# GpSimd makes the low parts of o's last 64 columns for nine pairs of heads in the middle of the output projection

## The reference, cut to what matters

```python
x = x + cross_attention(layernorm(x), ctx)      # 32 batches, 64 tokens, 16 heads of 64
x = x + rwkv_time_mix(layernorm(x), ...)        # k, v, r products, a scan over 64 tokens
x = x + feed_forward(layernorm(x), ...)         # 256 -> 1024 -> 256, relu
```

## Time and profile before

| | |
|---|---|
| median of 3 runs | 2353.97 us (2352.03 to 2357.43) |
| the profiled execution's own time | 2352.82 us |
| its span in the trace | 2351.0 us |
| PE busy | 2291.5 us, 97% of the span |
| DVE busy | 1812.6 us, 77% |
| ACT busy | 1542.7 us, 66% |
| POOL busy | 1646.7 us, 70% |

### The profile page before, as it was taken

How to read it: one execution, slowest core, us unless ns; L and a number is a source line. 1 busy time by engine, 2 the same in 40 slices (tenths; PEclk the granted TensorE clock), 3 DMA queues, 4 the chain that set the end, 5 groups by cost and what they waited for, 6 DMA issues and landing times.

```text
span 2351.0 us, 43942 instructions
## 1 busy us (share of the span) xinstructions
PE 2291.5 (97%) x13696; PEld 2097.1 (89%) x13696; DVE 1812.6 (77%) x3664; ACT 1542.7 (66%) x2696; POOL 1646.7 (70%) x858
## 2 busy tenths in 40 slices
PE   7979999999999999999999999999999999899999
PEld 5769999999999999999999999999999998878788
DVE  7867777777777777777777777777777777679884
ACT  6756666666666666666666666666666666565444
POOL 4238878888888888888888888888888886421111
PEclk9999999999999999999999999999999999999999
DMA  8988888888888888888888888888888886987000
GB/s 228 267 199 189 196 196 197 199 199 200 198 200 199 199 199 199 199 201 199 199 199 199 199 200 199 200 199 200 199 199 199 199 199 162 212 197 198 8 10 28
DMA packets 410273, 438.97 MB, mean 187 GB/s; under 512 B 82528, under 2 KB 380896, under 8 KB 410208
## 3 DMA queue, kind: packets, MB, share of 16 engines
q1 hardware_dynamic: 394384, 427.23, 77.3%
q10 hardware_dynamic: 15824, 10.91, 2.0%
HBM read 167.42 MB, written 52.43 MB: 94 GB/s over the span
## 4 chain that ended last, share of the span: by engine, by line
POOL 44%; issue 25%; PE 18%; SPq 5%; DVE 4%; DMA 2%; ACT 2%; POOLq 0%; ACTq 0%; DVEq 0%
POOL p_pt_lo L640 24%; POOL p_nat L667 7%; POOL p_q_lo L652 5%; POOL p_ct_lo L648 4%; POOL p_ct_hi L659 4%; SPq L441 3%; PE p_scores L1508 3%; PE p_scores L1678 2%; PE p_cols L1665 2%; PE p_scores L1632 2%; PE p_acc L1528 2%; PE p_cols L1574 2%; PE p_scores L1461 1%; DMA p_raw<-o_scratch 1%; PE p_scores L1590 1%
## 5 line engine op out<-in xcount | busy, mean ns | idle before, releaser
L640 POOL TENSOR_TENSOR p_pt_lo<-p_landed,p_pt_hi 128x768 fp32r<-128x768 f32 x504 | 991.1, 1987 | 322.7 <-ACT p_pt_hi L861 322.7
L1528 PE MATMUL p_acc<-p_nat,p_pt_hi 128*128 128x384 f32 x3024 | 887.6, 360 | 7.5 <-POOL p_pt_lo L640 5.7
L1530 PE MATMUL p_acc<-p_nat,p_pt_lo 128*128 128x192 f32 x3024 | 758.2, 251 | 0.0
L897 ACT ACTIVATE p_prob<-p_scores,p_negmax 128x800 f32<-128x800 f32 (+1 forms) x512 | 471.5, 926 | 392.8 <-DVE p_negmax L1222 392.7
L1508 PE MATMUL p_scores<-p_ct_hi,p_q_hi 128*128 128x512 f32 (+2 forms) x2048 | 703.6, 347 | 11.5 <-ACT p_prob L897 11.5
L1508 PE MATMUL p_scores<-p_ct_hi,p_q_lo 128*128 128x512 f32 (+2 forms) x2048 | 703.1, 347 | 0.0
L1528 PEld LDWEIGHTS p_acc<-p_nat,p_pt_hi 128*128 128x128 f32 x3024 | 567.4, 188 | 17.1 <-POOL p_pt_lo L640 10.1
L1530 PEld LDWEIGHTS p_acc<-p_nat,p_pt_lo 128*128 128x128 f32 x3024 | 577.0, 191 | 0.0
L861 ACT ACTIVATE p_pt_hi<-p_landed 128x768 fp32r<-128x768 f32 x504 | 398.6, 838 | 166.0 <-PE p_acc L1532 123.8
L1230 DVE STREAM_TRANSPOSE turned<-p_prob 128x1536 f32<-128x1536 f32 x256 | 452.5, 1768 | 0.0
L1508 PEld LDWEIGHTS p_scores<-p_ct_hi,p_q_hi 128*128 128x128 f32 x2048 | 389.0, 190 | 56.8 <-ACT p_prob L897 12.7
(11 more groups left out here) (229 smaller groups left out, 3126.2 us busy)
## 6 DMA issues: line engine op xcount, KB each, us to landing
p_landed<-turned SPq DMA_DIRECT2D x2032, 104.0 KB, 2.3
resid<-in_ctx SPq DMA_DIRECT2D x128, 288.0 KB, 5.0
o_scratch<-resid SPq DMA_DIRECT2D x256, 96.0 KB, 2.7
qk_scratch<-p_out_a SPq DMA_DIRECT2D x32, 512.0 KB, 5.1
p_stage<-qk_scratch SPq DMA_DIRECT2D x31, 512.0 KB, 3.8
p_stage<-qk_scratch SPq DMA_DIRECT2D x62, 256.0 KB, 4.2
p_stage<-in_ctxT SPq DMA_DIRECT2D x31, 401.0 KB, 4.7
p_stage<-in_ctxT SPq DMA_DIRECT2D x62, 200.5 KB, 5.6
```

The costliest lines, as they stand in the source:

```text
L640: nc.gpsimd.tensor_tensor(pt_lo[:, t0:t1, :, :], by_tile(slot, t0, t1), bits(pt_hi[:, t0:t1, :, :]), ALU.subtract).then_inc(pt_lo_done, 1)
L897: nc.scalar.activation(prob[:, lo:hi], scores[:, S0 + lo:S0 + hi], ACT.Exp, bias=negmax[:, par:par + 1], accum_out=rowsum[:, par, h:h + 1] ...
L1528: nc.tensor.matmul(acc[k % 2][:, 0:2 * DC], pt_hi[:, t, :, :].rearrange("p i x -> p (i x)"), x[:, t, :], start=t == 0, stop=False, skip_gr ...
L1530: nc.tensor.matmul(acc[k % 2][:, 0:DC], pt_lo[:, t, :, :].rearrange("p i x -> p (i x)"), x[:, t, 0:DC], start=False, stop=False, skip_grou ...
```

## The change

For the nine steps 13 to 21 the low part of `ob` is made on POOL instead of DVE. POOL does all nine between `to_mixed(0)` and `to_mixed(1)`, each as soon as `o_hi(n)` is done, and counts a new semaphore `ob_lo_done`. For these steps DVE's `o_lo(n)` is L1280 alone. Whoever waited for `o_lo_done` of such a step waits for both counters now: `v(n)` on PE and `load(n + 3)` on SP.

```diff
+        SHARED = range(13, 22)
+
+        def pair_split(eng, n):
+            eng.wait_ge(o_lo_done, n + 1)
+            if n in SHARED:
+                eng.wait_ge(ob_lo_done, n - SHARED.start + 1)
...
             def load(n):
-                sp.wait_ge(o_lo_done, n - RAW + 1)
+                pair_split(sp, n - RAW)
                 load_pair(sp, n)
...
+            def shared_lo(n):
+                s, r = n % 2, n % RAW
+                pool.wait_ge(o_hi_done, n + 1)
+                nc.gpsimd.tensor_tensor(ob_lo[s], ob[r], bits(ob_hi[s]), ALU.subtract).then_inc(ob_lo_done, 1)
+
-            to_mixed(0); to_mixed(1); to_x(2); to_x(3); to_mixed(2); to_fed(0); to_mixed(3); to_fed(1); to_fed(2); to_fed(3)
+            to_mixed(0)
+            for n in SHARED:
+                shared_lo(n)
+            to_mixed(1); to_x(2); to_x(3); to_mixed(2); to_fed(0); to_mixed(3); to_fed(1); to_fed(2); to_fed(3)
...
             def o_lo(n):
                 s, r = n % 2, n % RAW
                 dve.wait_ge(o_hi_done, n + 1)
-                nc.vector.tensor_tensor(oa_lo[s], oa[r], bits(oa_hi[s]), ALU.subtract)
-                nc.vector.tensor_tensor(ob_lo[s], ob[r], bits(ob_hi[s]), ALU.subtract).then_inc(o_lo_done, 1)
+                last = nc.vector.tensor_tensor(oa_lo[s], oa[r], bits(oa_hi[s]), ALU.subtract)
+                if n not in SHARED:
+                    last = nc.vector.tensor_tensor(ob_lo[s], ob[r], bits(ob_hi[s]), ALU.subtract)
+                last.then_inc(o_lo_done, 1)
...
             def v(n):
...
-                pe.wait_ge(o_lo_done, n + 1)
+                pair_split(pe, n)
```

More of the change, by code:

```diff
@@ L333, in whole_layer @@
         td_done, decay_done = sem("td"), sem("decay")
-        o_hi_done, o_lo_done = sem("o_hi"), sem("o_lo")
+        o_hi_done, o_lo_done, ob_lo_done = sem("o_hi"), sem("o_lo"), sem("ob_lo")
         v_ready, at_hi_done, at_lo_done, y_half, y_done, y_added = (sem(n) for n in ("v_ready", "at_hi", "at_lo", "y_half", "y_done", "y_added"))
@@ L1036, in load @@
                 else:
-                    act.wait_ge(o_lo_done, n - RAW + 1)
+                    pair_split(act, n - RAW)
                 load_pair(act, n)
```

## The result

| | before | after |
|---|---|---|
| median, 22 runs each | 2355.70 us (2352.03 to 2358.01) | 2358.52 us (2352.89 to 2366.45) |
| ratio | | 1.0013, 95% interval 1.0007 to 1.0019 |
| the profiled execution's span | 2351.0 us | 2359.5 us |

A forecast was written before the change was run, and what follows sets the result against it. PE was taken as the bound for steps 13 to 21, DVE from 2130 us. DVE's 0.9 us at step 21 plus 2.2 for the biases made 3.1, on 2353.97: 2357.1 us, range 2352.5 to 2361.5.

The forecast's parts named there:

- The bound: PE bounds steps 13 to 21 with 0.38 us to win at most; DVE bounds 2130.1 to 2155.9 us.
- DVE and POOL exclude each other: DVE instructions with two SBUF operands and POOL instructions run in turn: 1.14 + 1.25 us instead of 1.14 + 0.69.
- Steps 13 and 14, +0.6 on PE: v(13) starts 0.55 us later and v(14) 0.6, the same 0.6 and not a second one.
- Step 18, split 1.25 late: L1280 starts 1.85 us later, the split ends 1.25 later, and high parts 20 and 21 come 1.3 to 1.9 later.
- Steps 20 and 21: Another 0.65 us each for v, leaving v(21) about 1.5 late; DVE at at(19) 0.6 to 1.2 late, taken as 0.9.
- The biases pushed onto the recurrence, 2.2 us: to_mixed(1)'s four POOL instructions, queued behind the nine, alternate with DVE's recurrence: 4 x 0.54 = 2.2 us of DVE waiting.
- Downstream, carried whole: DVE is 3.1 us late from 2139 us on, PE catches up with that in waits, and the rest follows 3.1 us later.
- the one in which POOL is held off: Rival, chance 0.15: to_mixed(1) waits until DVE has a break, DVE pays only 0.9 to 1.5 us, about 2355.2.
- the one without exclusion: Rival, chance 0.06: all nine POOL instructions run beside DVE's; -0.4 us, about 2353.6.
- the full price: Rival, chance 0.17: each of nine steps hands on 0.65 us, 5.9 plus 2.2 = 8.1 us, 2362.1.
- one more drop of the clock: Rival, chance 0.10: new waits before v(20), v(21) or v(24) bring one PE clock drop, 1.7 us more, 2358.8.
- the signs named ahead: Trace signs: POOL's part within 0.1 us of L1280, about 2.4 us long; v(13) 0.55 later; biases over 4 us, scans 1.7.

The follow-up runs named there:

- the experiment made for it: Kernel before, with to_mixed(1) on POOL waiting until DVE has done key_value(0, 0), just as the first scan starts; run once for its trace, 2361.40 us.
- the steps that have slack: As the change, but POOL makes the low part for steps 15, 16, 17 and 19 alone, to_mixed(1) at its old time; ratio to before 0.9996 (0.9987 to 1.0005).

## Why the prediction was right

The time, 2357.1 forecast and 2358.52 measured, and the difference, 3.1 and 3.1 (1.6 to 4.5), agree. The time is 1.4 us above the forecast, and the median of before has moved by 1.7 the same way, from 2353.97 to 2355.70 with more runs. The terms agree less than the sum, and that the sum came out so close is partly luck: the 0.6 us on which the 0.9 for steps 13 to 21 was built did not come, and more came at steps 20 and 21.

- *The bound.* Right. PE was full before and stays so from step 14 to step 20; leaving the work out altogether was worth about a microsecond. The floor was taken too high, -0.4 us: A fell by 0.7 to 1.3. The nine extra waits, for which no row gave the 0.05 us each, cost nothing that shows: in the first trace of after `v(14)` to `v(19)` start within 0.01 us of the first of before.
- *DVE and POOL exclude each other.* Right, down to the length: 2.33 us where both come at once (2.4 forecast), or 2.20 on DVE's side, and 1.29 where POOL is alone.
- *Steps 13 and 14, +0.6 on PE.* Mis-sized, nearly nothing. `v(14)` to `v(19)` start 0.0 to 0.13 us late in the three traces against the first of before, and 0.03 to 0.26 against the second. The step that failed was the time of `v(13)`: it was read as waiting for its split, but PE was busy until it started, and `v(12)` came 0.4 us later in the second trace of before as in the three of after, so the first trace had `v(13)` early. It starts 6.63 and 6.94 us behind step 12 before, and 6.93 to 6.96 after. And at step 14 the 1.25 us of POOL were offset by two L1281 gone, not one: the large subtraction started 0.61 late and ended DVE's part of the split where it ended before (10.5 us behind step 12 in both).
- *Step 18, split 1.25 late.* Mis-sized: it started 1.03 late instead of 1.85, and without L1281 ended 0.43 late. The 0.6 of steps 13 and 14 was missing. The loads behind it were late about as forecast (1.3 to 1.9 us): against the first trace of before the high part of step 20 starts 0.8 to 1.4 us late, that of step 21 1.2 to 2.1, after waits of 1.5 to 3.3 us for the transfer.
- *Steps 20 and 21.* Right in size, a little low: the first scan came 0.64, 0.95 and 1.53 us late in three traces (0.9 forecast), against -0.53 to 0 in the four like before without the drop at `v(12)`; mean against mean it is 1.3. It came over the loads and not over PE: step 21's subtraction starts as its high part ends, which is 1.24, 1.55 and 2.13 us late, and the first scan follows it with one L1281 of 0.60 less between, which makes the 0.64, 0.95 and 1.53. And `v(21)` 1.1 to 2.0 (1.5 forecast), now waiting for POOL.
- *The biases pushed onto the recurrence, 2.2 us.* Right in the traces: 2.0 in three of them, gone when they are put back, 1.2 when they alone are moved and come 1 us ahead of the first scan. The times neither confirm nor refute it. This was the largest term and is not the cost of the moved instructions themselves; it came from asking what is queued behind them.
- *Downstream, carried whole.* Nearly: 3.3 us at step 22 (mean of three against the mean of two), 2.9 at the end, with the clock's drop behind the transposes' wait in one trace of either.

Of the rivals, the one in which POOL is held off fell with the experiment made for it, the one without exclusion with the first trace, the full price with the steps that have slack. (Its condition was miscounted: with 2.2 us from the biases, four steps at 0.65 already make 4.8 us, not five.) That of one more drop of the clock was the right cause of spread, but not through new waits. The new waits did come, 1.15 to 1.55 us before `v(21)` in all six traces with nine parts on POOL, and the clock dropped behind none of them; the drops happen in both kernels.

Of the signs named ahead, POOL's part starts 0.04 or 0.05 us behind L1296 at steps 13, 17, 20 and 21 and lasts 2.31 to 2.34 us, the biases and the scans are as said, and PE's wait before step 25 is 2.02 to 2.04 us. Only `v(13)` did not come 0.55 late.

## What to carry to other kernels

Before work is moved to an idle engine, look for two rows: an instruction of the old engine that is longer than its like while the new one runs, and the work that is queued behind the new instructions; here, by the traces, the second cost more than the first (2.0 and 1.3 us). Work taken from an engine that is not the bound is worth little, even when it is left out altogether: 1 to 1.5 us for 5.4 here. And when two kernels differ by a tenth of a per cent, count from a landmark just ahead of the edit, and look at the granted clock behind every wait before two stretches are compared: the recurrence repeated to 0.02 us in the traces of one kernel and the longer stretch A to 0.9, where the times of whole runs spread over 6 and more.

## What the runs showed of the hardware that was not expected

- GpSimd is kept out, and keeps out, by VectorE instructions with one SBUF tensor too, when they are of the tensor-by-scalars kind: four of 128 x 256 took 2.36 us beside a GpSimd instruction and 1.38 without. A reciprocal of one SBUF tensor was not touched: 3.32 us and 1.29 us side by side.
- Two engines that exclude each other took turns instruction by instruction also when VectorE's came back to back and first (1.71, 1.16, 1.23, 1.23 us for 1.22, 0.73, 0.74, 0.69). At 2250 us they did not, in any of thirteen traces: the VectorE instruction that was running and four behind it kept their lengths, and GpSimd's first took 3.53 us for the 0.70 that it has alone. What decides is open.
- TensorE waits at the same places in every trace, for 1.1 to 2.7 us each, but the clock's drop to the lower level came behind different ones from run to run, and cost 0 or 1.0 to 1.5 us by what was waited for next. It came behind the wait before `v(12)` in two traces of thirteen, and behind that before `v(21)` in none of six.
